# Carried state written into the first input column by ScalarE, and one tile of an input product on VectorE, in an image kernel with a selective scan

## The reference, cut to what matters

```
for t in range(L):                      # per image, 256 channels d, 16 states n
    dA  = exp(dt[t, d] * A[d, n])
    dBx = dt[t, d] * x[t, d] * B[t, n]
    h   = dA * h + dBx                  # h[d, n], starts at 0 for each image
    y[t, d] = sum_n h[d, n] * C[t, n] + x[t, d] * D[d]
out = silu(group_norm((y * silu(z)) @ W_out)) + input
```

## Time and profile before

| | |
|---|---|
| median of 3 runs | 14149.46 us (14147.47 to 14152.89) |
| the profiled execution | 14149.68 us, span 14147.8 us |
| busy share of the span | POOL 97%, DVE 96%, PE 79%, ACT 73% |
| granted TensorE clock, mean | 0.856 |
| DMA | 141 GB/s |

### The profile page before, as it was taken

How to read it: one execution, slowest core, us unless ns; L and a number is a source line. 1 busy time by engine, 2 the same in 40 slices (tenths; PEclk the granted TensorE clock), 3 DMA queues, 4 the chain that set the end, 5 groups by cost and what they waited for, 6 DMA issues and landing times.

```text
span 14147.8 us, 149910 instructions
## 1 busy us (share of the span) xinstructions
PE 11126.3 (79%) x32512; PEld 3271.3 (23%) x32512; DVE 13578.6 (96%) x11827; ACT 10277.8 (73%) x17321; POOL 13786.6 (97%) x3076
## 2 busy tenths in 40 slices
PE   6777777787777878778777778777787777877777
PEld 2222222222222222222222222222222222222221
DVE  7999999999999999999999999999999999999999
ACT  6777777777777777777777777777777777777776
POOL 7999999999999999999999999999999999999999
PEclk8888888888888888888888888888888888888887
DMA  5555565555555565555565555655555555656554
GB/s 130 143 138 142 140 150 137 143 136 145 144 143 145 134 147 140 146 137 142 139 147 143 139 144 136 149 140 143 138 141 141 146 143 137 143 140 149 138 141 113
DMA packets 1068166, 1991.27 MB, mean 141 GB/s; under 512 B 123650, under 2 KB 124731, under 8 KB 1067067
## 3 DMA queue, kind: packets, MB, share of 16 engines
q1 hardware_dynamic: 1065786, 1979.41, 57.8%
q10 hardware_dynamic: 1280, 0.02, 0.0%
HBM read 1626.62 MB, written 352.32 MB: 140 GB/s over the span
## 4 chain that ended last, share of the span: by engine, by line
POOL 64%; issue 35%; POOLq 0%; ACT 0%; PE 0%; DVE 0%; ACTq 0%; DMA 0%; SPq 0%; DVEq 0%
POOL hq L934 47%; POOL dbx L926 17%; POOLq L933 0%; ACTq L495 0%; DVE hq L825 0%; POOLq L925 0%; PE pp L318 0%; POOLq L923 0%; ACT ps_a L583 0%; DMA dt_d<-dt 0%; ACT pp L602 0%; PE pp L363 0%; DMA dt_rep<-dt_d 0%; ACT o L505 0%; POOLq L92 0%
## 5 line engine op out<-in xcount | busy, mean ns | idle before, releaser
L934 POOL TENSOR_TENSOR hq<-hq,c_rep 128x2048 f32<-128x2048 f32 x2048 | 9246.2, 4537 | 249.9 <-ACT carry L589 249.9
L825 DVE TENSOR_TENSOR_SCAN hq<-ps_a,carry,dbx 128x512 f32<-128x512 f32 x7168 | 8651.2, 1262 | 244.2 <-POOL dbx L926 89.8
L583 ACT ACTIVATE ps_a<-dt_rep,A_neg 128x512 f32<-128x512 f32 x8192 | 5564.6, 686 | 3396.0 <-DVE hq L825 3355.8
L926 POOL TENSOR_TENSOR dbx<-dtx_rep,b_rep 128x2048 f32<-128x2048 f32 x1024 | 4636.5, 4528 | 90.0 <-DMA dtx_rep<-dtx_d 90.0
L410 PE MATMUL ps_acc<-hq,dsum 128*32 128x512 f32 x16384 | 2426.5, 667 | 630.4 <-POOL hq L934 630.4
L812 DVE TENSOR_TENSOR dbx<-dtx_rep,ps_b 128x2048 f32<-128x2048 f32 x1024 | 2313.5, 2259 | 4.1 <-PE ps_b L398 4.1
L318 PE MATMUL pp<-xin,diag 128*128 128x504 f32 (+3 forms) x4608 | 2213.7, 608 | 6.0 <-ACT diag L615 6.0
L398 PE MATMUL ps_b<-dbl,bsel 41*128 41x512 f32 x2048 | 1306.9, 722 | 335.9 <-issue 172.9
L354 PE MATMUL pp<-x,W_taps 128*128 128x512 f32 x768 | 677.9, 981 | 731.0 <-DVE x L786 528.7
L825 DVE TENSOR_TENSOR_SCAN hq<-ps_a,dbx 128x512 f32<-128x512 f32 x1024 | 1187.4, 1205 | 46.6 <-ACT ps_a L583 31.7
L318 PEld LDWEIGHTS pp<-xin,diag 128*128 128x128 f32 x4608 | 793.1, 189 | 1398.3 <-issue 1398.3
(11 more groups left out here) (117 smaller groups left out, 10019.9 us busy)
## 6 DMA issues: line engine op xcount, KB each, us to landing
dtx_rep<-dtx_d SPq DMA_DIRECT2D x2048, 256.0 KB, 4.8
dt_rep<-dt_d SPq DMA_DIRECT2D x2048, 256.0 KB, 5.6
c_rep<-bc_d SPq DMA_DIRECT2D x1024, 256.0 KB, 5.4
b_rep<-bc_d SPq DMA_DIRECT2D x1024, 128.0 KB, 2.9
dtx_d<-sp SPq DMA_DIRECT2D x256, 512.0 KB, 2.8
dt_d<-dt SPq DMA_DIRECT2D x256, 512.0 KB, 6.0
out<-o SPq DMA_DIRECT2D x128, 512.0 KB, 4.0
xin<-in_x SPq DMA_DIRECT2D x192, 320.0 KB, 8.8
```

The lines of the kernel that those rows point to most:

```text
L583: A(ps_a[:, i % RA, :], dt_rep[:, q // NQ, g, :], ACT.Exp, scale=A_neg[:, q // NQ, q % NQ, g:g + 1]).then_inc(exp_done, 1)
L825: v.tensor_tensor_scan(hq[:, q % HQ, g, :], ps_a[:, i % RA, :], dbx[:, slot(q), g, :], carry[:, q, g:g + 1] if c % CH else 0.0, ALU.mult, ...
L926: g.tensor_tensor(dbx[:, slot(q), :, :], dtx_rep[:, d, :, :], b_rep[:, c % 2, q % NQ // 2, :].unsqueeze(1).to_broadcast([P, DG, T]), ALU.m ...
L934: g.tensor_tensor(quad, quad, c_rep[:, c % 2, q % NQ, :].unsqueeze(1).to_broadcast([P, DG, T]), ALU.mult).then_inc(cmul_done, 1)
```

## The change

The scan's start value becomes the constant 0.0 in every chunk. In chunks that are not the first of an image, ACT runs one instruction more for each tile, `add_carry`: it reads column 0 of the tile's exp from PSUM, multiplies it by the carried state (scale, through a pointer) and adds the first column of the input product (bias, through a pointer), and writes the result over that first column. The scan then waits for this instruction (`first_done`) and not for the exp. At step u ACT issues `add_carry` for tile u + 2, after the carry copy and before exp u + 3; at step 5 it also issues the one for tile 8, between the silus of xh and of z.

The second part: of group 7, the last one, the first of four tiles of the input product is made by DVE, at step 25, and POOL makes the other three. PE selects B once more for this (at step 24), and its selection for the next chunk's group 0 moves from step 24 to step 26. Some constants of the attention and the group norm move one step later.

```
-GN_STATS, GN_SUM, GN_MOM, GN_RSTD, GN_SCALE, GN_SILU = 24, 25, 25, 27, 27, 29
+GN_STATS, GN_SUM, GN_MOM, GN_RSTD, GN_SCALE, GN_SILU = 24, 25, 25, 27, 28, 29
-ATT_FC, ATT_H, ATT_MM, ATT_SUM, ATT_EXP, ATT_WTS = 24, 25, 26, 27, 29, 30
+ATT_FC, ATT_H, ATT_MM, ATT_SUM, ATT_EXP, ATT_WTS = 24, 25, 26, 28, 29, 31
+BY_DVE = (0, 2, 4, 6, 7)
+ND, SHARED, SPLIT = len(BY_DVE), 7, 1
...
 PE, chunk:
-                        if s + 2 < QUADS:
-                            select_b(b, c, s + 2)
-                        elif c + 1 < end:
-                            select_b(b, c + 1, 0)
+                        select_b(b, c, s + 2 if s + 2 < QUADS else SHARED)
+                    if u == 26 and c + 1 < end:
+                        select_b(b, c + 1, 0)
...
 ACT:
+            def add_carry(b, c, i):
+                q, g = divmod(i, DG)
+                m = (b * CH + c) * QUADS + q
+                if g == 0:
+                    if q % 2:
+                        act.wait_ge(bmul_pool, (b * CH + c) * (QUADS // 2) + q // 2 + 1)
+                    if q in BY_DVE:
+                        act.wait_ge(bmul_dve, (b * CH + c) * ND + BY_DVE.index(q) + 1)
+                    act.wait_ge(carry_done, m - QUADS + 1)
+                act.wait_ge(exp_done, (b * CH + c) * NT + i + 1)
+                first = dbx[:, slot(q), g, 0:1]
+                A(first, ps_a[:, i % RA, 0:1], ACT.Identity, scale=carry[:, q, g:g + 1], bias=first).then_inc(first_done, 1)
...
 ACT, chunk:
+                    if u + 2 < NT:
+                        if c % CH and u != ACT_XZ + 1:
+                            add_carry(b, c, u + 2)
+                    elif c + 1 < end and (c + 1) % CH:
+                        add_carry(b, c + 1, u + 2 - NT)
...
                         if c + 1 < end:
                             silu_xh(b, c + 1, 0)
                             silu_xh(b, c + 1, 1)
+                        if c % CH:
+                            add_carry(b, c, u + 3)
                         silu_z(b, c, 0)
                         silu_z(b, c, 1)
...
 DVE:
+                m = SPLIT if q == SHARED else DG
+                v.tensor_tensor(dbx[:, slot(q), 0:m, :], dtx_rep[:, d, 0:m, :],
+                                ps_b[:].unsqueeze(1).to_broadcast([P, m, T]), ALU.mult).then_inc(bmul_dve, 1)
...
+                if c % CH:
+                    dve.wait_ge(first_done, ((b + c // CH) * (CH - 1) + c % CH - 1) * NT + i + 1)
+                else:
+                    dve.wait_ge(exp_done, (b * CH + c) * NT + i + 1)
                 v.tensor_tensor_scan(hq[:, q % HQ, g, :], ps_a[:, i % RA, :], dbx[:, slot(q), g, :],
-                                     carry[:, q, g:g + 1] if c % CH else 0.0, ALU.mult, ALU.add).then_inc(scan_done, 1)
+                                     0.0, ALU.mult, ALU.add).then_inc(scan_done, 1)
...
 DVE, chunk:
+                    if u == 25:
+                        weigh_inputs(b, c, SHARED)
...
 POOL:
+                m = SPLIT if q == SHARED else 0
+                g.tensor_tensor(dbx[:, slot(q), m:, :], dtx_rep[:, d, m:, :],
+                                b_rep[:, c % 2, q % NQ // 2, :].unsqueeze(1).to_broadcast([P, DG - m, T]),
                                 ALU.mult).then_inc(bmul_pool, 1)
```

More of the change, by code:

```diff
@@ L176, in build_program @@
         wait_taken, kept, att_step, a_loaded = sem("wait_taken"), sem("kept"), sem("att_step"), sem("a_loaded")
+        first_done = sem("first_done")
         dt_repd = [sem("dt_repd_0"), sem("dt_repd_1")]
@@ L250, in spread_dtx @@
                 if not (isinstance(b, int) and b * CH + c == 0):
-                    sp_e.wait_ge(bmul_dve, (b * CH + c - 1) * (QUADS // 2) + 2 * (d + 1))
+                    sp_e.wait_ge(bmul_dve, (b * CH + c - 1) * ND + sum(q // NQ <= d for q in BY_DVE))
                     sp_e.sem_inc(wait_taken, 1)
@@ L393, in select_b @@
             def select_b(b, c, q):
-                n = (b * CH + c) * (QUADS // 2) + q // 2
+                n = (b * CH + c) * ND + BY_DVE.index(q)
                 pe.wait_ge(dbl_done, b * CH + c + 1)
@@ L548, in evac_dbl @@
                     act.wait_ge(bc_out, 16 * (b * CH + c - 1))
-                    act.wait_ge(bsel_mm, (b * CH + c - 1) * (QUADS // 2))
+                    act.wait_ge(bsel_mm, (b * CH + c - 1) * ND)
                 A(dbl[0:NDBL, c % 2, :], pp[0:NDBL, 0, :], ACT.Copy).then_inc(dbl_done, 1)
@@ L805, in weigh_inputs @@
                 d = q // NQ
-                dve.wait_ge(bsel_mm, (b * CH + c) * (QUADS // 2) + q // 2 + 1)
+                dve.wait_ge(bsel_mm, (b * CH + c) * ND + BY_DVE.index(q) + 1)
                 if q % NQ == 0:
@@ L809, in weigh_inputs @@
                 n = (b * CH + c) * QUADS + q
-                if not (isinstance(n, int) and n < 2):
+                if q == SHARED:
+                    dve.wait_ge(scan_done, DG * (n - 3))
+                elif not (isinstance(n, int) and n < 2):
                     dve.wait_ge(scan_done, DG * (n - 1))
-                v.tensor_tensor(dbx[:, slot(q), :, :], dtx_rep[:, d, :, :],
-                                ps_b[:].unsqueeze(1).to_broadcast([P, DG, T]), ALU.mult).then_inc(bmul_dve, 1)
+                m = SPLIT if q == SHARED else DG
+                v.tensor_tensor(dbx[:, slot(q), 0:m, :], dtx_rep[:, d, 0:m, :],
+                                ps_b[:].unsqueeze(1).to_broadcast([P, m, T]), ALU.mult).then_inc(bmul_dve, 1)
             def scan(b, c, i):
@@ L818, in scan @@
                 if g == 0:
-                    dve.wait_ge(bmul_pool if q % 2 else bmul_dve, (b * CH + c) * (QUADS // 2) + q // 2 + 1)
+                    if q % 2:
+                        dve.wait_ge(bmul_pool, (b * CH + c) * (QUADS // 2) + q // 2 + 1)
+                    if q in BY_DVE:
+                        dve.wait_ge(bmul_dve, (b * CH + c) * ND + BY_DVE.index(q) + 1)
                     if not (isinstance(m, int) and m < HQ):
                         dve.wait_ge(sum_done, m - HQ + 1)
-                    if c % CH:
-                        dve.wait_ge(carry_done, m - QUADS + 1)
-                dve.wait_ge(exp_done, (b * CH + c) * NT + i + 1)
+                if c % CH:
+                    dve.wait_ge(first_done, ((b + c // CH) * (CH - 1) + c % CH - 1) * NT + i + 1)
+                else:
+                    dve.wait_ge(exp_done, (b * CH + c) * NT + i + 1)
                 v.tensor_tensor_scan(hq[:, q % HQ, g, :], ps_a[:, i % RA, :], dbx[:, slot(q), g, :],
-                                     carry[:, q, g:g + 1] if c % CH else 0.0, ALU.mult, ALU.add).then_inc(scan_done, 1)
+                                     0.0, ALU.mult, ALU.add).then_inc(scan_done, 1)
             def group_stats(b):
@@ L925, in weigh_inputs @@
                     pool.wait_ge(scan_done, DG * (n - 3))
-                g.tensor_tensor(dbx[:, slot(q), :, :], dtx_rep[:, d, :, :],
-                                b_rep[:, c % 2, q % NQ // 2, :].unsqueeze(1).to_broadcast([P, DG, T]),
+                m = SPLIT if q == SHARED else 0
+                g.tensor_tensor(dbx[:, slot(q), m:, :], dtx_rep[:, d, m:, :],
+                                b_rep[:, c % 2, q % NQ // 2, :].unsqueeze(1).to_broadcast([P, DG - m, T]),
                                 ALU.mult).then_inc(bmul_pool, 1)
```

## The result

The changed kernel takes 14300.44 us (median of 4 runs, 14299.15 to 14301.57), the kernel before beside it 14149.14 (4 runs, 14147.47 to 14152.89). The ratio is 1.0105, interval 1.0093 to 1.0117: slower by 151 us. The forecast was 14092 and its range ended at 14275, so both the direction and the range were wrong. The profiled execution has a span of 14297.3 us and a mean granted clock of 0.856, as before.

A forecast was written before the change was run, and what follows sets the result against it. DVE's own queue was taken to bound six of eight chunks, POOL only c = 4. Chunk terms summed to 436.65 us an image against 438.5, -57 over 31 images, so 14092 us from 14149.68; range 13960 to 14275.

The forecast's parts named there:

- What bounds the kernel: Whole kernel: DVE's own queue sets the time in six of eight chunks; POOL is the bound only in c = 4.
- Scans: DVE scans lose their pointer operand: 0.06 us gained each, 1.92 us a chunk, in seven chunks of eight.
- Split product: Group 7's first input product tile moves to DVE, adding 0.58 us to its queue a chunk.
- POOL's saving: POOL's shorter fourth input product saves 1.12 us a chunk, lowering its floor from 53.83 to 52.71.
- the add's price: Each one-column add on ACT lasts 0.33 us and takes 0.235 us of ACT's queue.
- Places A, B, C: A: chunk end, before scan 0, 1.2 us stall; B: steps 5-9, 0.96; C: steps 9-13 in c = 1-4, 0.23.
- It is due only after scan 29, three scans on, so that costs nothing in a plain chunk: PE's select for the next chunk, moved from step 24 to 26 behind the new product: no cost in plain chunks.
- 62.3: Forecast length in us of c = 8, the group norm chunk without adds, against about 63.35 before.
- 56.6: Forecast length in us of c = 5, the attention chunk, against 58.35 before, including about 2.2 waiting for PE's heads.
- R2: Rival, 27%: ACT's queue becomes the bound at steps 9 to 24, scans 12, 13, 16, 21, 24 late; 14274 us.
- R3: Rival, 4%: the pointer is not what the 0.06 us a scan is; 14505 us.
- R1: Rival, 17%: POOL stays the bound, adds cheap or hidden, the places give little; 13910 at best, up to 14030 us.

The follow-up runs named there:

- zero start: The kernel before with every scan started from 0.0 and no adds, so state is not carried between chunks: 14116.95 us, ratio 0.9976.
- Root first: The early split with the reciprocal root at step 29 put ahead of the next chunk's first exp, behind add 31: 14036.12 us, ratio 0.9920.
- early split: The changed kernel with DVE's split product at step 23, not 25, and PE's selections at steps 22 and 25: 14148.13 us, ratio 0.9999.
- without the adds: The sums late kernel with the pointer back, no adds, and the root back behind the exp: 14087.45 us, ratio 0.9956.
- sums late: The Root first kernel with DVE's attention sums at step 30 instead of 28: 13983.31 us, ratio 0.9882.
- adds-only kernel: The kernel before plus ACT's adds and scans from 0.0; POOL makes all of group 7's product, selection at step 24: 14305.18 us, ratio 1.0110.
- free adds: The changed kernel with adds issued on unused columns, not waiting for input products, scans released by the exp, state not carried: 14194.95 us, ratio 1.0032.

## Why the prediction was wrong

**What bounds the kernel.** Right: DVE's queue in most chunks and POOL in c = 4. The zero start shows both at once.

**Scans.** Right: 0.06 us each, 1.115 apart. **Split product, POOL's saving, the add's price.** Right to 0.03 us each.

**Places A, B, C.** Right: 1.16, 0.84 and 0.16 against 1.2, 0.96 and 0.23. (The terms listed for place C add up to 5.0 and not 5.05, which gives 0.18.) c = 7, which has no place A, came at 51.91 against 51.8. *Root first* cleared place A and took 1.1 us off c = 2 (53.30 to 52.22), which confirms its price.

**The step that failed: "It is due only after scan 29, three scans on, so that costs nothing in a plain chunk"**, and with it "62.3" for c = 8 and "56.6" for c = 5. I asked when the moved selection's result is due, and not what stands behind it in PE's queue. In the plain chunk c = 2 the step held to 0.1 us; it failed where other work stood behind the selection. In c = 8 that was the variance, then ACT's ln, then the group silus. I had DVE's wait for these grow by nothing, because the silus "move up 1.1"; they came later, and the wait grew from 35.7 us in all to 104.2, or by 2.1 an image. In c = 5 I did count the select before the heads, at 2.2 us of waiting; the average is 3.6 (115.5 / 32), and the chunk misses by 1.4. The wait for the product (0.54 in the image read) and the selection's 2.07 are what I had put (1.1 and 1 to 2); but DVE asked for the heads only 0.8 later behind PE's product before them (4.06 us after, 3.25 before), where I had 1.7. The early split changes this order and little else, and takes back 4.5 of the 6.5 us. So PE's order around the new product is shown as the cause of those 4.5. PE also works at the lower of its two clock levels there; the early split's own trace parts the two in c = 5 (see the last section).

**The other 2 us an image.** In c = 1, 0.9 is left after the early split. There ACT starts its loop over images anew. Its first carry copy after that, and PE's first convolution product behind ACT:

```profile
7248.02 0.21 ACT L606 ACTIVATE carry<-hq 128x4 f32<-128x4 f32 x1 [2.16 <-DVE hq L856]
...
7250.09 2.07 PE L359 MATMUL pp<-x,W_taps 128*128 128x512 f32 x2 [10.90 <-ACT x L637]
```

The copy comes 2.06 us after scan 0, which is also the median over the images; in the kernel before it came 0.61 ahead of it (median). It goes with the adds: *without the adds* the copy is ahead again, by 0.47, and c = 1 takes 53.12, as its neighbours do. Why ACT restarts late was not tried. In c = 8 the early split still stands 0.8 over the forecast, and so does *sums late*: DVE now waits for PE's group sums, 31.3 us in all or 1.0 an image, a wait that the changed kernel does not have.

**R2** named the right side and nearly the right time (14274), but by luck, since its mechanism is not there: its waits before scans 12, 16, 21 and 24 are not in the changed kernel, and an add costs 0.25 of the queue where R2 needed 0.27. Its cousin is in the adds-only kernel (scans 26, 28, 29). **R3** is out. **R1** did not happen; its condition, that the places give little, was met only after they were cleared, and then the time was 13983.

**The parts were not independent.** I added the split (+0.58 of DVE) and the adds' places as if each had a price of its own. The split's 0.58, and POOL's shorter product, cover 0.6 of ACT's lateness in a plain chunk. In the sum of the changed kernel this did no harm, since I had not counted that lateness at all.

## What to carry to other kernels

When an instruction is moved in a queue that runs in order, its own due time is half of the question: list what is queued behind it until the queue next has slack, and who waits for that, through the second and third engine. Here one product and two selections stood one to two steps too late, on an engine that was busy 80%, and cost 152 us. And judge a change by its places before its busy time: with every price as before, five moves (the product, two selections, the root, the sums) turned 1.05% slower into 1.2% faster.

## What the runs showed of the hardware

A lower TensorE clock stood with the new wait, but in the image read here it was there before PE had waited. PE in c = 8 of the changed kernel, first the wait before the moved selection, then the work behind it; below them the work from the D products to the variance in the kernel before:

```profile
7668.71:7670.04 1.33, 0.01 (x1) 0.00 (x0) 1.33 (x3) 0.59 (x1) 1.33 (x2) 0.51 1.08 283
7670.04:7676.90 6.86, 6.86 (x18) 1.57 (x22) 6.66 (x10) 3.00 (x8) 6.26 (x2) 0.60 1.06 220
```

```profile
7587.30:7594.00 6.70, 3.56 (x15) 0.98 (x14) 5.38 (x12) 4.06 (x11) 6.70 (x3) 0.98 0.81 187
```

After, PE is busy all 6.86 us at a granted clock of 0.60, near the lower level (1.2 GHz); before, it had 3.56 us of work at 0.98, near the upper (2.4 GHz). Two D products took 2.07 us after and 1.10 before. But the clock stood at 0.51 during the wait already, so the wait did not bring it down here. The mean clock over the span is 0.856 in both kernels, and over the whole of c = 8 it is 0.86 after and 0.82 before, so neither shows it.

In c = 5 the D products and the state sum ran at the lower level in the kernel before as well. After, with the selection in front:

```profile
7505.31 2.07 PE L403 MATMUL ps_b<-dbl,bsel 41*128 41x512 f32 x2 [0.54 <-DVE dbx L839]
7507.32 2.08 PE L412 MATMUL ps_acc<-xh,D_diag 128*128 128x512 f32 x2
7509.32 1.94 PE L415 MATMUL ps_acc<-hq,dsum 128*32 128x512 f32 x8
...
7512.08 0.17 DVE L779 TENSOR_TENSOR att<-pp,w_spke_b 128x13 f32<-128x13 f32 x1 [3.46 <-PE pp L312]
```

The *early split* has no wait before this selection, and its trace has both levels. The same work, from the selection to the heads, in c = 5 of two of its images:

```profile
8743.29:8747.70 4.41, 4.41 (x20) 1.56 (x18) 4.34 (x8) 4.34 (x13) 4.41 (x1) 1.00 1.07 218
7425.87:7431.83 5.96, 5.96 (x18) 1.72 (x16) 3.92 (x4) 5.70 (x16) 5.72 (x2) 0.59 1.06 224
```

DVE does not wait for the heads in the first and waits 2.15 us in the second. Over 28 images the selection ran at the upper level in 13, with a mean wait of 0.60, and at the lower in 15, with 2.62; in the changed kernel it ran at the lower in all, with 3.49. So in c = 5 the order is worth about 0.9 us at the same level, and the level itself another 2.0. In c = 8 the order is nearly all: the silus' wait is 3.49 in the changed kernel, and in the early split 0.86 in the images at the lower level and 0.62 in the others. What makes the level fall in one image and not in the next no run shows.

And the add's price: the Trainium skill ("ScalarE: Activation LUTs", What ACT_TABLE_LOAD costs) makes it 186 ns and about 93 for each of two pointers, 372 ns, an estimate from that page; measured 350, with its source in PSUM, and 382 in *free adds*, with all operands in SBUF.
